# One gather a round handed from GpSimd to single-row fetches by SyncE, and node features laid out 56 to a partition: a graph layer on one Trainium2 core

## What is computed

```python
msg  = relu(x[src] + edge_attr @ We + be)           # 200000 x 128
aggr = segment_sum(msg, dst, num_segments=6250)
h    = (1 + eps) * x + aggr
h    = relu(h @ W1 + b1) @ W2 + b2
h    = (h - mean(h)) * rsqrt(var(h) + 1e-5) * gamma + beta   # over the nodes
out  = layernorm(x + relu(h) + x)                   # over the 128 features
```

## Time and profile before

| | |
|---|---|
| median of 3 runs | 1559.09 us (1558.66 to 1559.86) |
| the profiled execution | 1564.18 us, its span 1562.2 us |
| PE busy | 1416.0 us (91%) |
| ACT busy | 1255.7 us (80%) |
| POOL busy | 1160.5 us (74%) |
| DVE busy | 891.9 us (57%) |
| DMA | 180.72 MB, mean 116 GB/s |

### The profile page before, as it was taken

One profiled execution on the slowest core, in us unless ns is written; L12 is line 12 of the kernel. 1 busy time (PEld: TensorE's weight loads), 2 busy tenths in 40 slices (PEclk: granted clock), 3 DMA queues, 4 the chain that ended last, 5 costly groups with the idle time before them and its releaser, 6 DMA issues.

```text
span 1562.2 us, 60471 instructions
## 1 busy us (share of the span) xinstructions
PE 1416.0 (91%) x23435; PEld 1095.0 (70%) x23435; DVE 891.9 (57%) x3174; ACT 1255.7 (80%) x3729; POOL 1160.5 (74%) x1193
## 2 busy tenths in 40 slices
PE   1299999999999999989999999989999999999954
PEld 1277777777777777767777777767777777777734
DVE  5676665655566565555555556555556555655436
ACT  2488888888888888878877888878788888888845
POOL 7677777777777777777777777777777777777762
PEclk9999999999999999999999999999999999999967
DMA  9644445444544445444444444445444444444432
GB/s 250 170 111 109 109 113 123 113 111 117 119 113 110 108 112 126 109 106 113 111 108 106 113 106 113 112 106 117 108 110 107 111 112 107 105 112 110 104 125 84
DMA packets 148516, 180.72 MB, mean 116 GB/s; under 512 B 41725, under 2 KB 128980, under 8 KB 147972
## 3 DMA queue, kind: packets, MB, share of 16 engines
q1 hardware_dynamic: 102489, 89.62, 24.5%
q0 software_dynamic: 37728, 77.31, 20.9%
q10 hardware_dynamic: 8011, 9.90, 2.3%
HBM read 170.09 MB, written 6.63 MB: 113 GB/s over the span
## 4 chain that ended last, share of the span: by engine, by line
PE 55%; POOL 21%; issue 8%; ACT 5%; DVE 4%; DMA 4%; SPq 1%; ACTq 0%; POOLq 0%; DVEq 0%
POOL xg L590 21%; PE ps L1396 20%; PE ps L1381 14%; PE ps L1325 9%; PE ps L1311 6%; DMA xg<-xb,idxb 3%; ACT hot L747 2%; ACT msg L753 1%; PE ps L1362 1%; ACT hot L740 1%; PE ps L1342 1%; PE ps L1365 1%; PE ps L1334 1%; PE ps L1337 1%; SPq L480 1%
## 5 line engine op out<-in xcount | busy, mean ns | idle before, releaser
L590 POOL DMA_INDIRECT xg<-xb,idxb x1145 | 1107.0, 967 | 356.9 <-issue 337.0
L1396 PE MATMUL ps<-iota_all 128*128 128x128 bf16 x8064 | 518.0, 220 | 0.0
L1396 PEld LDWEIGHTS ps<-iota_all 128*128 128x128 bf16 x8064 | 452.3, 98 | 87.1 <-issue 67.7
L984 DVE TENSOR_TENSOR msg<-ps,xg 128x512 f32<-128x512 f32 x390 | 264.5, 688 | 305.6 <-DMA xg<-xb,idxb 192.8
L707 ACT ACTIVATE iota_all<-ps 128x384 bf16<-128x384 f32 x896 | 379.8, 484 | 31.7 <-PE ps L1381 28.4
L740 ACT ACTIVATE hot<-iota,rel 128x64 f32<-128x64 f32 x1560 | 391.6, 339 | 0.0
L1381 PE MATMUL ps<-x,iota_all 112*32 112x384 bf16 x7168 | 365.1, 331 | 0.0
L1069 DVE TENSOR_TENSOR accT<-accT,ps 128x64 f32 x390 | 86.2, 221 | 292.4 <-PE ps L1342 248.1
L753 ACT ACTIVATE msg<-msg 128x512 f32<-128x512 f32 x390 | 241.0, 618 | 14.7 <-DVE msg L984 14.7
L1381 PEld LDWEIGHTS ps<-x,iota_all 112*32 112x32 bf16 x7168 | 156.9, 96 | 120.6 <-issue 38.5
L1325 PE MATMUL ps<-msg,hot 128*64 128x128 f32 x3120 | 219.4, 284 | 23.1 <-ACT msg L753 23.1
(11 more groups left out here) (145 smaller groups left out, 800.3 us busy)
## 6 DMA issues: line engine op xcount, KB each, us to landing
ea<-in_eat SPq DMA_DIRECT2D x156, 320.0 KB
lowB<-lowD SPq DMA_DIRECT2D x128, 224.0 KB
xg<-xb,idxb POOLq DMA_INDIRECT x1145
accT<-in_xt ACTq DMA_DIRECT2D x1, 3125.0 KB, 14.8
x<-in_xt ACTq DMA_DIRECT2D x1, 3125.0 KB, 11.0
out<-iota_all SPq DMA_DIRECT2D x5, 512.0 KB
iota_all<-in_x ACTq DMA_DIRECT2D x3, 784.0 KB, 17.6
xb<-iota_all SPq DMA_DIRECT2D x3, 784.0 KB, 16.8
```

What stands on the lines that cost most here:

```text
L590: pool.indirect_dma_start(out=xg[0:rows, slot, j, :], out_offset=None, in_=of, in_offset=bass.IndirectOffsetOnAxis(ap=index, axis=0)).then ...
L984: add = dve.tensor_tensor(both, lin_of(half), xg[:, g % RING, :, :].rearrange("p (b t) h -> p b (t h)", b=2), ALU.add)
L1396: last = pe.matmul(found[:, e, :], sel2[set_of(k)][:, t, e * P:(e + 1) * P], rows3[:, t, a, :], start=(t == 0 and e == 0 and a == 0), stop ...
```

## The change

It has two parts.

1. **Layout of x.** Node n is in partition n // 56, block n mod 56. So a piece of x (14 blocks) is one run of 7168 bytes in each of 111 partitions, and the 112th partition, which holds only 34 nodes, has a small DMA of its own in three of the four pieces. This holds for the load (ScalarE's queue) and for the store to `xb` (SyncE's queue). `split_sources`, `nodeu` and the index in `pick` follow the new order; the first products of batch 0 wait for three of the four pieces of `x3` at once, where they waited for two.
2. **Fetch.** In rounds 1 to 12, group 3 has only 3 tiles gathered by GpSimd. The fourth is fetched by SyncE as 128 DMAs of one row (512 bytes) each during the round before: in each of its 15 steps, after `spread_lows`, 9 indices are loaded into registers and 9 DMAs issued (2 in the last step). The rows land in `xs`, a buffer of two tiles. `add_x` of that group waits for them and is three instructions, for 1, 1 and 2 tiles.

```diff
+    LASTP = SUB - 1
+    LASTR = N - LASTP * NSUB
...
+    FETCH_G = 3
+    FETCH_ROWS = 9
...
+        xs = sb("xs", [P, 2, HID])
+        idxs = sb("idxs", [1, 2, P], i32)
...
+        def fetched(i, g):
+
+            return i > 0 and g == FETCH_G
+
         def by_pool(i, g):
 
-            return GROUP - HALF * special(i, g)
+            return GROUP - HALF * special(i, g) - fetched(i, g)
...
-                sp.dma_start(xb[a * SUB:whole * SUB, :].rearrange("(b p) h -> p b h", p=SUB), xrow[0:SUB, a:whole, :])\
+                sp.dma_start(xb[0:LASTP * NSUB, :].rearrange("(p b) h -> p b h", b=NSUB)[:, a:b, :], xrow[0:LASTP, a:b, :])\
                   .then_inc(s_xb[q], 16)
-                if whole < b:
-                    sp.dma_start(xb[whole * SUB:N, :], xrow[0:N - whole * SUB, whole, :]).then_inc(s_xb[q], 16)
+                if a < last:
+                    sp.dma_start(xb[LASTP * NSUB + a:LASTP * NSUB + last, :].rearrange("(p b) h -> p b h", p=1),
+                                 xrow[LASTP:SUB, a:last, :]).then_inc(s_xb[q], 16)
+
+            def load_sources(i):
+
+                e0 = (i * ROUND + FETCH_G) * GE + (GROUP - 1) * P
+                sp.dma_start(idxs[:, i % 2, :], src_row[:, e0:e0 + P]).then_inc(s_idxs, 16)
+
+            def fetch(i, a, b):
+
+                if a == 0:
+                    wait_apart(sp, s_idxs, 16 * i)
+                    if i == 1:
+                        for m in range(NQ):
+                            sp.wait_ge(s_xb[m], stores(m))
+                    if i >= 3:
+                        wait_apart(sp, s_pre, (i - 2) * ROUND + FETCH_G + 1)
+                _, node_of = nc.values_load_multi_w_load_instructions(
+                    idxs[0:1, i % 2, a:b], engines=[mybir.EngineType.SP], min_val=0, max_val=N - 1,
...
+                for p in range(a, b):
+                    sp.dma_start(xs[p:p + 1, i % 2, :], xb[bass.ds(node_of[p - a], 1), :]).then_inc(s_row[i % 2], 16)
...
                     for j, k in phase(i, q, 3):
                         spread_lows(j, k)
+                    if i + 1 < ITERS:
+                        fetch(i + 1, q * FETCH_ROWS, min(P, (q + 1) * FETCH_ROWS))
+                    if q == STEPS - 1 and i + 2 < ITERS:
+                        load_sources(i + 2)
...
-                act.dma_start(xrow[0:SUB, a:whole, :], x[a * SUB:whole * SUB, :].rearrange("(b p) h -> p b h", p=SUB))\
+                act.dma_start(xrow[0:LASTP, a:b, :], x[0:LASTP * NSUB, :].rearrange("(p b) h -> p b h", b=NSUB)[:, a:b, :])\
...
-                both = to.rearrange("p (b t) h -> p b (t h)", b=2)
-                add = dve.tensor_tensor(both, lin_of(half), xg[:, g % RING, :, :].rearrange("p (b t) h -> p b (t h)", b=2),
-                                        ALU.add)
+                if fetched(i, g):
+                    dve.wait_ge(s_row[i % 2], 16 * P * ((i + 1) // 2))
+                    dve.tensor_tensor(to[:, 3, :], ps_lin(half, 3), xs[:, i % 2, :], ALU.add)
+                    dve.tensor_tensor(to[:, 2, :], ps_lin(half, 2), xg[:, g % RING, 2, :], ALU.add)
+                    add = dve.tensor_tensor(to[:, 0:2, :].rearrange("p t h -> p (t h)"), lin_of(half)[:, 0, :],
+                                            xg[:, g % RING, 0:2, :].rearrange("p t h -> p (t h)"), ALU.add)
...
-                    pe.wait_ge(s_rest[1], min(NQ, max(2, -(-2 * PAIRS * (t + 1) // PIECE))))
+                    pe.wait_ge(s_rest[1], min(NQ, -(-(NPAIR + PAIRS * (t + 1)) // PIECE)))
```

More of the change, by code:

```diff
@@ L100, in gine_layer_kernel @@
     CLOSE = 11
+    FETCH_G = 3
+    FETCH_ROWS = 9
+    assert FETCH_ROWS * STEPS >= P and FETCH_G not in SORTED
     BANKS = (3, 7, 4)
@@ L300, in gine_layer_kernel @@
         s_last = sem("s_last")
+        s_idxs = sem("s_idxs")
+        s_row = [sem("s_row_even"), sem("s_row_odd")]
         s_pro = sem("s_pro")
@@ L347, in stores @@
         def stores(q):
-            return 16 * (1 + (q == NQ - 1 and N % SUB > 0))
+            return 16 * (1 + (PIECES[q][0] < LASTR))
         block = ctx.enter_context(nc.Block())
@@ L498, in keep_lifted @@
                 a, b = PIECES[q][0], sum(PIECES[q])
-                whole = min(b, N // SUB)
+                last = min(b, LASTR)
                 sp.wait_ge(s_lifted, q + 1)
-                sp.dma_start(xb[a * SUB:whole * SUB, :].rearrange("(b p) h -> p b h", p=SUB), xrow[0:SUB, a:whole, :])\
+                sp.dma_start(xb[0:LASTP * NSUB, :].rearrange("(p b) h -> p b h", b=NSUB)[:, a:b, :], xrow[0:LASTP, a:b, :])\
                   .then_inc(s_xb[q], 16)
-                if whole < b:
-                    sp.dma_start(xb[whole * SUB:N, :], xrow[0:N - whole * SUB, whole, :]).then_inc(s_xb[q], 16)
+                if a < last:
[14 more added lines that the diff above has]
+                    idxs[0:1, i % 2, a:b], engines=[mybir.EngineType.SP], min_val=0, max_val=N - 1,
+                    skip_runtime_bounds_check_because="each is the src of an edge, a row of x")
+                for p in range(a, b):
+                    sp.dma_start(xs[p:p + 1, i % 2, :], xb[bass.ds(node_of[p - a], 1), :]).then_inc(s_row[i % 2], 16)
             def spread_lows(j, k):
@@ L655, in _ @@
                 a, b = PIECES[q][0], sum(PIECES[q])
-                whole = min(b, N // SUB)
-                act.dma_start(xrow[0:SUB, a:whole, :], x[a * SUB:whole * SUB, :].rearrange("(b p) h -> p b h", p=SUB))\
+                last = min(b, LASTR)
+                act.dma_start(xrow[0:LASTP, a:b, :], x[0:LASTP * NSUB, :].rearrange("(p b) h -> p b h", b=NSUB)[:, a:b, :])\
                    .then_inc(s_xrow[q], 16)
-                if whole < b:
-                    act.dma_start(xrow[0:N - whole * SUB, whole, :], x[whole * SUB:N, :]).then_inc(s_xrow[q], 16)
+                if a < last:
+                    act.dma_start(xrow[LASTP:SUB, a:last, :],
+                                  x[LASTP * NSUB + a:LASTP * NSUB + last, :].rearrange("(p b) h -> p b h", p=1))\
+                       .then_inc(s_xrow[q], 16)
             act.dma_start(accT[:, 0:N], xt).then_inc(s_xt, 16)
@@ L876, in _ @@
             step(dve.memset(epsc[:, 0:1], EPS))
-            step(dve.memset(xrow[:, NSUB - 1, :], 0.0))
+            step(dve.memset(xrow[LASTP // 32 * 32:SUB, LASTR:NSUB, :], 0.0))
             dve.wait_ge(s_we, 16 * 6)
@@ L954, in constants @@
                 dve.tensor_scalar(starts[:, :], iota[:, 0:NPAIR], float(CAP), None, ALU.mult)
[L955 to L956 removed]
+                dve.tensor_scalar(nodeu[:, 0:1], nodes[:, 0:1], 2.0, None, ALU.mult)
+                dve.tensor_scalar(nodeu[:, 1:2], nodes[:, 0:1], 2.0, 1.0, ALU.mult, ALU.add)
             def split_sources():
                 dve.wait_ge(s_srcT, 1)
[L960 removed]
+                pair = float(NPAIR)
                 source = ps[:, 3:7, :].rearrange("p a n -> p (a n)")[:, 0:LOOPED * GROUP]\
                     .rearrange("p (m c) -> p m c", c=CYCLE)[:, :, CYCLE - HALF:CYCLE]
[L963 removed]
+                step(dve.tensor_scalar(near, source, 0.5 - pair / 2, 1.0 / pair, ALU.add, ALU.mult))
                 step(dve.tensor_scalar_add(part_of, near, 12582912.0))
                 step(dve.tensor_scalar_add(part_of, part_of, -12582912.0))
[L966 to L968 removed]
+                dve.tensor_copy(low_of.rearrange("p (m c) -> p m c", c=HALF), part_of)
+                step(dve.scalar_tensor_tensor(out=near, in0=part_of, scalar=-pair, in1=source, op0=ALU.mult, op1=ALU.add))
+                step(dve.tensor_scalar(start_of.rearrange("p (m c) -> p m c", c=HALF), near, float(CAP), None, ALU.mult))
             dve.nop().then_inc(s_tr, 1)
@@ L982, in add_x @@
                 to = msg[:, q % TURN, half * GROUP:(half + 1) * GROUP, :]
-                both = to.rearrange("p (b t) h -> p b (t h)", b=2)
-                add = dve.tensor_tensor(both, lin_of(half), xg[:, g % RING, :, :].rearrange("p (b t) h -> p b (t h)", b=2),
-                                        ALU.add)
+                if fetched(i, g):
[4 more added lines that the diff above has]
+                                            xg[:, g % RING, 0:2, :].rearrange("p t h -> p (t h)"), ALU.add)
+                else:
+                    both = to.rearrange("p (b t) h -> p b (t h)", b=2)
+                    add = dve.tensor_tensor(both, lin_of(half), xg[:, g % RING, :, :].rearrange("p (b t) h -> p b (t h)", b=2),
+                                            ALU.add)
                 if isinstance(i, int) and i == 0 and g < UNBIASED:
```

6 lines of the change are left out of this document (4 added, 2 removed).

## The result

The changed kernel takes 1848.07 us (median of 4 runs, 1845.83 to 1851.55) against 1558.88 us before in the same session: a ratio of 1.1857, 95% interval 1.1835 to 1.188, or 289 us more. The profiled execution's span is 1844.9 us. The forecast was 1592 us, 1576 to 1690. The direction was right; the likeliest case was not the one that happened, and the rival that did happen (SyncE's queue as the bound) was priced too low for the range to hold it.

The account below looks back on a forecast made before the run. Bound by TensorE first, GpSimd's gathers in the middle, both nearly together from about 1176 us. 1564.2 + 47.1 (start) - 14 (gathers) + 0 (SP) = 1597.3, less 5.1 to the median: 1592 us, range 1576 to 1690.

Parts of the forecast that it names:

- the likeliest case: Whole kernel: x moves on three DMA engines, the fetch costs SP nothing; 1592 us, own range 1581 to 1620, chance 0.48.
- the rival that did happen (SyncE's queue as the bound): Loop: SP's commands become the bound; 1628 us at 0.40 us a row, some 1710 at 0.459; chance 0.33.
- xb complete at 105 us, +47.1: Start: x moves on three DMA engines, so `xb` completes at 105 us instead of 57.9; bounds +37 to +74.
- The 20.5 us from `xb` to the loop: Start: the time from `xb` complete to VectorE's first `add_x` stays 20.5 us.
- -14 us for 12 gathers: Loop: GpSimd loses 12 gathers of 1.273 us; between 12.1 and 15.3 us saved, 14 taken.
- SP's round, 60.5 + 128 c = 105.3 us, cost 0: Loop: SP's work a round, c = 0.35 us to issue a one-row DMA, covered by 538.2 us of `lowS` waits.
- The rest, 39.6 us: SP's old work a round: `lowD`, its landing, `lowB`, edge-feature loads, index lists and 0.5 us for the remainder.
- the two signs of being wrong: Loop: a row costing over 0.37 us, or VectorE waiting for `lowB`, would show SP's cover gone.
- its rule from SP's round to the time: Loop: 9.5 rounds times SP's round above 107.2 us, less 7 us, by group 286; more after it.
- c = 0.459: Loop: a one-row DMA's issue as dear as the 106-row store's; SP's round 119.3 us, some 1710 us in all.
- The spread layout as a gain of 12.9 us: Start: x's DMAs use all engines and longer runs help; `xb` at 45 us, -12.9, 1532 us in all; chance 0.13.
- The Trainium skill's price of a DMA: SP's queue: 512 cycles, an estimated 0.43 us a DMA; round 115.5 us, some 70 us above the forecast sum.

Follow-up runs that it names:

- experiment 3: Kernel before, with its 512-byte runs, but each piece of x loaded and stored as 111 partitions and 1 partition: 1629.72 us, ratio 1.046.
- experiment 4: Changed kernel without the fetch, each piece of x loaded and stored as 96, 15 and 1 partitions: 1557.55 us, ratio 1.0004.
- experiment 5: Kernel before plus the fetch, but SyncE loads nine node numbers into registers once and uses them for all 1536 rows: 1542.73 us, ratio 0.9903.
- experiment 8: Kernel before plus the fetch at eight rows a step, issued between `lowD` and `lowB` in steps with a batch: 1544.45 us, ratio 0.99.
- experiment 10: Kernel before plus the fetch, rows between `lowD` and `lowB`, two DRAM copies of `lowD`: ten rows a step 1551.69 us, eight rows 1542.8 us.
- experiment 2: Kernel before plus the fetch, with the old layout of x: 1796.14 us, ratio 1.1529.
- experiment 7: Kernel before plus the fetch, thinned: six rows a step (8 tiles in the run) 1548.93 us, eight rows a step (12 tiles) 1598.07 us.
- experiment 9: Kernel before plus the fetch at ten rows a step, 14 tiles, issued between `lowD` and `lowB`, one copy of `lowD`: 1643.5 us, ratio 1.053.

## Why the prediction was right or wrong

**xb complete at 105 us, +47.1.** Right in mechanism and within its bounds (+37 to +74), low by 9 us: GpSimd went on 56.4 us later. Three engines: the window at 0.19 and 79 GB/s shows it, experiments 3 and 4 that 111 is the cause. The Trainium skill's rule (DMA: Bandwidth & Descriptors, "Why a DMA increments its semaphore by 16 and not by 1") agrees with all four cases: 112, 111, 96 with 15, and the 106 rows of the last store. What was off was the mean rate: (6.36 / 3 + 0.53) MB in 113 us is 23.5 GB/s an engine, for the 25.5 that was taken. Where the three work alone they reach it (79 / 3.04 = 26, 100 to 110 us), so the 9 us were lost earlier, for instance from 45 to 60 us, where all engines are busy at 275 GB/s, 17 an engine. Whether slower transfers or pauses made it isn't told apart.

**The 20.5 us from `xb` to the loop.** Right: 114.32 to 134.62 us.

**-14 us for 12 gathers.** Right, where SP doesn't bind: 15 to 16 us in experiments 5, 8 and 10 (with eight rows), a little over the 12.1 to 15.3 that were given.

**SP's round, 60.5 + 128 c = 105.3 us, cost 0.** This is the step that failed. It was 130.6 us, 25 more. By its terms: a row took (3.57 - 0.23) / 8 = 0.417 us from start to start in a group of nine, against 0.396, which is +2.7 us a round. The DMA itself was cheaper than the lowest bound (0.228 us against 0.306), but there are two more commands and three gaps with it; in that the term was right by luck. The 15 loads of registers were taken at 1.0 us each and took 25 us a round (four at 0.95, ten at 2.07, the short one at 0.65), +10. The rest, 39.6 us, was some 12 us too low: `lowD` lands in 284.1 / 114 = 2.5 us instead of 2.32, which is about 2 us of the 12. The others are not waits for engines, since SP had none in this stretch; they are mostly gaps between commands, which the sum of medians leaves out (on SP's timeline from 800 to 830 us 0.2 us stand before each `lowD` and 0.4 us before a list of indices that follows edge features). The mean of 1.0 us was read off a row that said otherwise: 864/1089/2314 ns holds loads of two kinds, and the median shows one.

Of the two signs of being wrong that the prediction named for this step, one came: VectorE waited 221.1 us for `lowB`. The other, a row above 0.37 us, hardly did. Less the register operation that the term counts apart, a row took 0.417 - 0.046 = 0.371 us, which alone would have made a round of 108.0 us, at the edge of what is covered. So it was the loads and the old work that decided, not the price of a row.

**The rival's price.** Its mechanism is what happened, and its rule from SP's round to the time holds closely. Put experiment 2's 131.1 us into it: 9.5 x (131.1 - 107.2) - 7 = 220 us by group 286, and 2.5 x (131.1 - 115) = 40 after it, 260 in all. Measured were 1796.1 us, 252 us over the 1544 that the hidden fetch takes. The rival was stopped at c = 0.459, as if the issue of a DMA were the only thing unknown; the loads and the old work were treated as known. Had the loads been let go to the longest of their row (2.314 us) as c was to its longer ones, the same sum would have given 39.6 + 34.7 + 128 x 0.505 = 138.9 us a round, and a range up to there holds the result.

**The spread layout as a gain of 12.9 us.** Wrong in its size: experiment 4 made the layout spread, and it gained nothing. The Trainium skill's figure of 512 bytes for line rate (DMA: Bandwidth & Descriptors, "Specifications"), against which the forecast held 391 GB/s, was the better guide where all engines work: run length changed nothing in the time there. On three engines it wasn't: `xb` was complete at 114.3 us with runs of 7 KB and at 129.3 with runs of 512 bytes, and there the measurement decides. The rival had also priced the last store at 8 us as if the engines were free; it landed 21.6 us after the last lift. The two rates of the trace belonged to two transfers that differ in more than their runs.

**The Trainium skill's price of a DMA,** 512 cycles or an estimated 0.43 us (DMA: Bandwidth & Descriptors, the passage on faster descriptor generation), is not what the DMA command of a row took here: 0.228 us, and 0.294 with the two register commands before it. With the gaps it is 0.417 us from row to row. Its total, some 1662 us, was nearer than the forecast, and still 186 us short.

## What to carry to other kernels

Before a partition is taken out of a DMA, look at the divisors of what is left: 112 to 111 cost 56 to 71 us here, and 96 + 15 + 1 gave it back. A queue that "only waits" has a budget like any engine: add up its commands with their gaps and the landings that it waits for, compare the sum with the pace of the loop, and fill its waits for landings before moving work elsewhere (54 us here, by the order of commands alone). Ask which waits that makes longer: with ten rows the wait came back for another landing and cost 92 us. Where a row shows a minimum and a maximum far apart, find out what makes the two kinds before using the median.

## What was not expected of the hardware

A TENSOR_LOAD of nine words into SP's registers took 0.95 us where the address was a multiple of 16 bytes (every fourth step, at a stride of 36 bytes) and 2.07 us elsewhere. In the changed kernel the load that starts at 804.7 us took 2.070 us and the one at 826.7 took 0.949. The timeline of SP shows both as the distance from the end of the command before to the first row: 806.91 - 804.62 = 2.3 us, and 827.83 - 826.65 = 1.2 us. Nine numbers are loaded in each; the last line counts six rows since the view ends there.

```profile
804.25 0.37 SPq L488 DMA_DIRECT2D idxb<-in_src_loop  x1
806.91 3.57 SPq L539 DMA_DIRECT2D xs<-xb  x9
...
826.30 0.35 SPq L552 DMA_DIRECT2D lowB<-lowD  x1
827.83 2.35 SPq L539 DMA_DIRECT2D xs<-xb  x6
```

Loads of eight words at aligned addresses took 0.72 us, less than the 0.91 for six (experiment 7):

```profile
L547 SPq TENSOR_LOAD <-idxs x176: 664/913/1166, 82.1 to 1363.5; - x176
```

An estimate that fits these rows, if four aligned words are one access and every other word is one of its own: 0.39 us and 0.187 us for each access, from the nine words at both addresses ((2.07 - 0.95) / 6, with three accesses and nine). It gives 0.76 for eight words (two accesses, 0.72 measured) and 0.95 for six (three accesses, 0.91 measured). For ten at a stride of 48 bytes (four accesses) it gives 1.14, and 1.20 was measured (experiment 9); for the two of a round's last step it gives 0.76, where 0.65 was measured, so it is rough. That this is how the loads are made was not tested further.
